# A ring of seven PSUM banks shared by scores and mean transposes, V loaded whole for the last tile, and one shared tile for the left-over keys

## The reference

```python
# first attention (L0), 4 heads of 32: only the 32 best keys of a row count
scores = einsum(Q, K) / sqrt(32)                 # 4 x 1024 x 6404
topv, topi = top_k(scores, 32)
attn = zeros.at[topi].set(softmax(topv))
attn_mean = attn.mean(axis=heads)                # 1024 x 6404
c_t = attn_mean @ V                              # 1024 x 128
...
# second attention (L1), 16 heads of 8: plain softmax over all 6404 keys
attn = softmax(q @ k.T / sqrt(8)); out = attn @ v
```

## Time and profile before

| | us |
|---|---|
| median of 3 runs | 2005.47 (2000.84 to 2008.52) |
| the profiled execution, its own time | 2001.17 |
| its span in the trace | 1999.4 |
| loop of the first attention | about 205 to 861 of the span |
| second attention | about 1076 to 1809 of the span |
| granted TensorE clock, mean | 0.9 |

### The profile page before, as it was taken

One profiled execution on the slowest core, in us unless ns is written; L12 is line 12 of the kernel. 1 busy time (PEld: TensorE's weight loads), 2 busy tenths in 40 slices (PEclk: granted clock), 3 DMA queues, 4 the chain that ended last, 5 costly groups with the idle time before them and its releaser, 6 DMA issues. The chain is left out here.

```text
span 1999.4 us, 22599 instructions
## 1 busy us (share of the span) xinstructions
PE 1590.6 (80%) x8229; PEld 609.5 (30%) x8229; DVE 857.4 (43%) x2286; ACT 1387.5 (69%) x1382; POOL 177.6 (9%) x153
## 2 busy tenths in 40 slices
PE   4357978888788788356464999999999999995996
PEld 3236334445444455333220111111111111113332
DVE  5734699999899898836320000000000000003223
ACT  3471678778778787410224999999999999992432
POOL 2743021111111111100000000000000000000000
PEclk8566989999999999678666999999999999997998
DMA  2122086796786876767002000610070000003000
GB/s 86 51 92 97 11 163 150 165 209 144 172 193 136 196 166 157 167 110 113 21 12 37 1 1 1 56 14 1 7 64 1 1 1 1 1 1 91 0 0 11
DMA packets 91348, 145.08 MB, mean 73 GB/s; under 512 B 46704, under 2 KB 59465, under 8 KB 90433
## 3 DMA queue, kind: packets, MB, share of 16 engines
q0 software_dynamic: 13472, 75.53, 18.9%
q1 hardware_dynamic: 77328, 67.19, 15.7%
q10 hardware_dynamic: 432, 0.85, 0.1%
HBM read 54.15 MB, written 13.99 MB: 34 GB/s over the span
## 5 line engine op out<-in xcount | busy, mean ns | idle before, releaser
L1735 ACT ACTIVATE ex<-ps 128x1536 f32<-128x1536 f32 x544 | 731.2, 1496 | 1.2 <-PE ps L1694 1.0
L1707 PE MATMUL ps<-ex,V 128*9 128x512 f32 x3264 | 427.3, 596 | 0.2 <-ACT ex L1735 0.2
L753 PE MATMUL ps<-K,qst 128*128 128x512 f32 (+1 forms) x832 | 380.3, 601 | 20.6 <-ACT srow L819 14.7
L1694 PE MATMUL ps<-Q,K 52*128 52x512 bf16 x1632 | 328.9, 385 | 64.9 <-ACT ex L1735 33.3
L1745 DVE COPY o<-ps 9x512 f32<-9x512 f32 x32 | 22.0, 687 | 742.8 <-PE ps L1707 742.0
L947 DVE MAX8 cand<-srow 128x8 f32<-128x200 f32 (+1 forms) x1024 | 320.8, 363 | 8.0 <-ACT srow L819 8.0
L819 ACT COPY srow<-ps 128x1024 f32<-128x1024 f32 (+1 forms) x224 | 206.0, 922 | 98.8 <-PE ps L753 98.2
L907 DVE SCALAR_TENSOR_TENSOR both<-srow,top,both 128x1536 f32<-128x1536 f32 (+1 forms) x128 | 240.1, 1876 | 42.5 <-ACT both L835 42.3
L835 ACT ACTIVATE both<-srow,shift 128x1536 f32<-128x1536 f32 (+1 forms) x128 | 209.0, 1636 | 10.5 <-DMA both<-both 9.4
L753 PEld LDWEIGHTS ps<-K,qst 128*128 128x128 f32 x832 | 157.9, 201 | 177.1 <-issue 139.1
L1694 PEld LDWEIGHTS ps<-Q,K 52*128 52x128 bf16 x1632 | 60.2, 94 | 482.0 <-ACT ex L1735 446.8
(11 more groups left out here) (306 smaller groups left out, 1064.0 us busy)
## 6 DMA issues: line engine op xcount, KB each, us to landing
both<-both POOLq DMA_DIRECT2D x69, 768.0 KB, 8.8
v_ring<-v_rows SPq DMA_DIRECT2D x96, 256.0 KB, 3.9
both<-both POOLq DMA_DIRECT2D x23, 898.0 KB, 12.6
K<-k_parts SPq DMA_DIRECT2D x48, 204.0 KB
k_parts<-kl SPq DMA_DIRECT2D x12, 384.0 KB, 2.5
V<-v_rows SPq DMA_DIRECT2D x4, 918.0 KB, 30.8
v_rows<-v1g SPq DMA_DIRECT2D x12, 288.0 KB, 3.0
v_rows<-V SPq DMA_DIRECT2D x12, 256.0 KB, 3.2
```

Source lines behind the costliest of these rows:

```text
L753: last = M.matmul(ps[:, GBANK * (k % RING) + b, 0:c1 - c0], qst[:, h, :], K0[:, c0:c1], start=True, stop=True)
L1694: last = M.matmul(ps[:, n % 6, :], K1[rows_, quad % 2, hh // 2, g * P:(g + 1) * P], Q1[rows_, 4 * quad + hh, tb * TB:(tb + 1) * TB], start ...
L1707: last = M.matmul(ps[32 * j:32 * j + VW, 6 + w % 2, :], V1[:, quad % 2, g, VW * j:VW * j + VW], ex1[:, (4 * g + j) % NSLOT, :], start=g == ...
L1735: C.activation(ex1[:, n % NSLOT:n % NSLOT + NBANK, :], ps[:, n % 6:n % 6 + NBANK, :], ACT.Exp)\
```

## The change

1. **Ring.** Score groups and transposes share one ring of 7 banks. An order of all items (`ITEMS`: score group k, then the transposes that follow it) is written out at build time, with the bank of each (`BANK_OF`) and the number of items that ACT must have copied before it may be written (`FREE_AT`). While transposes follow every score group, this comes to: score group k waits for the copy of group k - 2; a transpose waits for the copy of a transpose or group at least one step back.
2. **Schedule.** The 13 transposes of tiles 0 to 5 follow 13 score groups in a row (offsets 3 to 15) instead of every second. `value_group` j comes 3 score groups behind its transposes (offsets 6 to 18), and `meanT` has 4 slots. `HURRIED` keeps its offsets for the transposes; its products also come 3 later.
3. **Whole V.** For tile 7 SP loads 50 tiles of V, 3.2 MB in rows of 25.6 KB, with one DMA into the slot of `srow` that turn 29 has freed. It stands in SP's queue ahead of the last two loads of tile 6, and waits for the last mask of turn 29. In the tail the transposes go up to 7 groups ahead, and the products run 3 groups behind them.
4. **Shared tile of keys.** In the second attention the 4 left-over keys of four heads share one tile, in 32 partitions each: 201 tiles and 67 units a pass. The last unit has 2 full score matmuls and 4 small ones; the last two value groups of a pass (49 and 50) fall into the same unit, unit 1 of the next pass. `load_quad` loads V in 1 + 4 DMAs.

```diff
-    RING = 3
+    RING = 7
+    MSLOTS = 4
+    VALUE_LAG = 3
+    TAIL_LAG = 3
-    SPREAD = [3, 5, 7, 9, 11, 13, 15, 17, 19, 21, 23, 24, 25]
+    SPREAD = list(range(3, 3 + NTURN))
...
+            TURN_AT[k] = (u, i)
+            VALUE_AT[k + VALUE_LAG] = (u, i)
+    ITEMS = []
+    for k in range(NI * NGRP):
+        ITEMS.append(("scores", k))
+        if k in TURN_AT:
+            ITEMS.append(("turn", TURN_AT[k]))
+    BANK_OF, FREE_AT, at, held = [], [], 0, {}
+    for n, (kind, k) in enumerate(ITEMS):
+        size = min(GBANK, NBK - (k % NGRP) * GBANK) if kind == "scores" else 1
+        if at + size > RING:
+            at = 0
+        BANK_OF.append(at)
+        FREE_AT.append(max(held.get(b, 0) for b in range(at, at + size)))
+        for b in range(at, at + size):
+            held[b] = n + 1
+        at += size
...
 def scores(n, g):
-                    if k >= RING:
-                        pe.wait_ge(S("evac"), k - RING + 1)
+                    if FREE_AT[item]:
+                        pe.wait_ge(S("evac"), FREE_AT[item])
...
 def turn_group(u, j):
-                    if m >= 1:
-                        pe.wait_ge(S("meanT_sb"), m if u < NT - 1 or j == 0 else m - 1)
+                    if u < NT - 1:
+                        pe.wait_ge(S("evac"), FREE_AT[ITEM_AT["turn", (u, j)]])
+                    elif j >= RING:
+                        pe.wait_ge(S("tail_copied"), j - RING + 1)
...
 for n in range(NI): for g in range(NGRP):
                         scores(n, g)
-                        mean_step(n * NGRP + g)
+                        k = n * NGRP + g
+                        if k in TURN_AT:
+                            turn_group(*TURN_AT[k])
+                        if k in VALUE_AT:
+                            value_group(*VALUE_AT[k])
...
 @block.sync
+                    if m == IN_TAIL - 2:
+                        sp.wait_ge(S("kept"), kept_by(LAST - 2, LOW))
+                        sp.dma_start(srow[:, (LAST - 2) % SLOTS, 0:(NG - 1) * P],
+                                     v0_rows[:, 0:NG - 1, :].rearrange("p n d -> p (n d)")).then_inc(S("v0_whole"), 16)
                     if m >= 2:
                         sp.wait_ge(S("summed"), m - 1)
...
 def load_quad
-        sp.dma_start(V1[:, b, :, :], v1_rows[:, :, quad * 4 * VW:(quad + 1) * 4 * VW]).then_inc(values_in, 16)
+        sp.dma_start(V1[:, b, 0:FULL1, :], v1_rows[:, 0:FULL1, quad * 4 * VW:(quad + 1) * 4 * VW]).then_inc(values_in, 16)
+        for j in range(4):
+            h0 = (4 * quad + j) * VW
+            sp.dma_start(V1[LEFT * j:LEFT * (j + 1), b, FULL1, 0:VW], v1_rows[0:LEFT, FULL1, h0:h0 + VW]).then_inc(values_in, 16)
...
-        NU = 4 * NG // NBANK
+        NTILE = 4 * FULL1 + 1
+        NU = NTILE // NBANK
...
 def scores(w, u)
+                        for hh in ([n % 4] if g < FULL1 else range(4)):
+                            if g < FULL1:
+                                out, col = ps[:, bank(w, n), :], 0
+                                keys = slice(g * P, (g + 1) * P)
+                            else:
+                                out, col = ps[LEFT * hh:LEFT * (hh + 1), bank(w, n), :], LEFT * hh
+                                keys = slice(g * P, g * P + LEFT)
```

More of the change, by code:

```diff
@@ L673, in program @@
         for i in range(NTURN):
[L674 to L676 removed]
+            k = first + (SPREAD if u < NT - 2 else HURRIED)[i]
+            TURN_AT[k] = (u, i)
+            VALUE_AT[k + VALUE_LAG] = (u, i)
+        SUMS_AT[k + VALUE_LAG + 1] = u
+    ITEMS = []
[3 more added lines that the diff above has]
+            ITEMS.append(("turn", TURN_AT[k]))
+    ITEM_AT = {item: n for n, item in enumerate(ITEMS)}
+    BANK_OF, FREE_AT, at, held = [], [], 0, {}
[8 more added lines that the diff above has]
+        at += size
     DEEP = 3
@@ L728, in edge_by, with evac_by, v0_tile @@
             return n * STEPS + 8
+        IN_TAIL = (NT - 1) * NTURN
         def turn_bank(m):
-            return 6 if m < (NT - 1) * NTURN else 5 + m % 2
+            return BANK_OF[ITEM_AT["turn", divmod(m, NTURN)]] if m < IN_TAIL else (m - IN_TAIL) % RING
+        def evac_by(k):
+            return ITEM_AT["scores", k] + 1
+        def v0_tile(u, c):
+            if u == NT - 1 and c < NG - 1:
+                return srow[:, (LAST - 2) % SLOTS, c * P:(c + 1) * P]
+            return v0_ring[:, (u * NTURN + c // 4) % 2, c % 4, :]
         def home_free(eng, n, c):
@@ L778, in value_group @@
                         w = min(P, G - c * P)
-                        last = M.matmul(ps[:, 7, 0:D], meanT[0:w, m % 2, (c % 4) * P:(c % 4 + 1) * P],
-                                        v0_ring[0:w, m % 2, c % 4, :], start=c == 0, stop=c == NG - 1)
+                        last = M.matmul(ps[:, 7, 0:D], meanT[0:w, m % MSLOTS, (c % 4) * P:(c % 4 + 1) * P],
+                                        v0_tile(u, c)[0:w, :], start=c == 0, stop=c == NG - 1)
                     last.then_inc(S("summed"), 1)
[L783 to L791, removed]
                 for n in range(NI):
@@ L817, in evac @@
                     act.wait_ge(S("scored"), n * NGRP + g + 1)
-                    b = GBANK * ((n * NGRP + g) % RING)
-                    C.copy(srow[:, n % SLOTS, g0:g1], ps[:, b:b + GBANK, :].rearrange("p a b -> p (a b)")[:, 0:g1 - g0])\
+                    b = BANK_OF[ITEM_AT["scores", n * NGRP + g]]
+                    C.copy(srow[:, n % SLOTS, g0:g1],
+                           ps[:, b:b + -(-(g1 - g0) // 512), :].rearrange("p a b -> p (a b)")[:, 0:g1 - g0])\
                         .then_inc(S("evac"), 1)
@@ L1179, in program @@
     KIN = 12
+    FULL1 = G // P
+    LEFT = 32
+    VIN = 1 + 4
+    assert NG == FULL1 + 1 and G - FULL1 * P <= LEFT
     oq, k1s = ExitStack(), ExitStack()
@@ L1706, in values @@
                     for j in range(4):
-                        last = M.matmul(ps[32 * j:32 * j + VW, 6 + w % 2, :], V1[:, quad % 2, g, VW * j:VW * j + VW],
-                                        ex1[:, (4 * g + j) % NSLOT, :], start=g == 0, stop=g == NG - 1,
-                                        tile_position=(0, 32 * j))
+                        out = ps[32 * j:32 * j + VW, 6 + w % 2, :]
+                        if g < FULL1:
+                            last = M.matmul(out, V1[:, quad % 2, g, VW * j:VW * j + VW], ex1[:, slot(w, 4 * g + j), :],
+                                            start=g == 0, stop=False, tile_position=(0, 32 * j))
+                        else:
+                            left = slice(LEFT * j, LEFT * (j + 1))
+                            last = M.matmul(out, V1[left, quad % 2, g, 0:VW], ex1[left, slot(w, NTILE - 1), :],
+                                            start=False, stop=True, tile_position=(LEFT * j, 32 * j))
                     last.then_inc(S("summed1"), 1)
```

106 lines of the change are left out of this document (63 added, 43 removed).

## The result

**Slower, by 1.3%.** The changed kernel takes 2030.91 us (median of 4 runs, 2024.38 to 2035.49) where the kernel before took 2005.4 (median of 4, 2000.84 to 2008.52): ratio 1.0127, 95% interval 1.0091 to 1.0162. I had forecast 2003, with a range of 1980 to 2023; this is the side of rival 2, between its 2019 and its 2036.

What follows compares the result with a forecast made beforehand. DVE was taken to set the pace in the first attention's turns 5 to 29, ACT in the second attention. Terms +3.8 - 2.6 + 5 - 7 - 3.8 + 2 = -2.6 us took the median 2005.5 to 2003; range 1980 to 2023.

Steps and rivals of the forecast that it cites:

- rival 2: Turns with consecutive steps: PE becomes the bound through late loads or half clock; 2019 to 2036 us, chance 0.30.
- the term +3.8: Six tiles, turns 5 to 29: new load stalls of 37.2 us against 33.4 us saved, net +3.8 us.
- The same stall is thus only moved: Six tiles: the old stall in turn 4u+7 moves to turn 4u+6, at 6.2 us a tile.
- 33.4 taken away and 37.2 added: Six tiles: the mean's 33.4 us cost to DVE goes; load stalls of 6.2 us a tile add 37.2.
- M(5) to M(29) over 483: Sign of rival 2: first masks of turns 5 and 29 start 483 us or more apart, against 470 forecast.
- Rival 1: Six tiles: loads of V get through the adds earlier, stall 3.4 us; total 1986 us, chance 0.33.
- Turns 29 to 31: +2.4 forecast: First mask of turn 29 to that of turn 31: -2.6 us and +5 us together, +2.4 us.
- The term of 5: Turns 29 to 31: whole V among the adds delays ACT's exponentials, +5 us, from 0 to 9.
- the term of -2.6: Turn 29 to 30: little mean work left and hurried loads in a quiet stretch, 18.05 for 20.7 us, -2.6 us.
- Tail: -7: From the last add to the first loop's end: transposes and first products already done, -7 us, between -10 and -4.
- Second attention: -3.8: Second attention: 8 fewer exponentials, -10.8 us, against ACT gaps of 6.0 and a later end of 1.0; -3.8 us.
- Loads for it: +2: Stage before the second attention: eight more small DMAs ahead of x_sb in SP's queue, +2 us, from 0 to 4.

Runs made afterwards that it cites:

- e2: Changed kernel with the old table of offsets, transposes after every second score group; 1975.23 us, ratio 0.9848 to the kernel before.
- e1: Changed kernel with the 89 ring loads of V left out, products reading two slots loaded once (computation incomplete); 1973.51 us, ratio 0.9853 to before.
- e10: Changed kernel with adds of every first added head cut to 8 columns a chunk (computation incomplete); 1964.2 us, ratio 0.9798 to before.
- e7: Changed kernel with the whole V issued behind the last load of tile 6 and the last mask of turn 30; 2027.75 us.
- e4: Kernel before with only the shared key tile added, including its loads of V in 1 + 4 DMAs; 2005.96 us, ratio 1.0011.
- e8: Changed kernel with the old table of offsets and x_sb loaded ahead of V and the keys; 1972.11 us, ratio 0.985 to before.
- e12: Changed kernel with the old table of offsets and the second attention of before; 1977.8 us, ratio 0.9872 to before.
- e3: Changed kernel with x_sb loaded ahead of the loads for the second attention; 2026.28 us, ratio 1.0138 to before.

## Why the prediction was wrong

1. **The stall of a tile: the term +3.8 measured +22.9.** This is the step that failed. I had put the new stall at 6.2 us a tile, 37.2 for six, over the 433.3 without a mean; it measured 489.6 - 433.3 = 56.3, or 9.4 a tile. The step was wrong in two places.
   - *Which load is late.* I followed products 8, 10 and 12 and let the odd loads through. The rows had the landing times about right (5.6, 9.4; measured 5.9, 7.6, 9.6, 7.9), but with a step of 3 us four loads in a row, 7 to 10, are issued into the adds. Load 9 took 9.6 us, and product 9 is the one ahead of the scores (8,2). I had put the stall on the last mask of turn 6, at 6.2 us; it came on the first, at 9.1 us in tile 0. The two half-clock pieces, 1.4 and 1.3 us in the scores alone, had no term, only a sentence.
   - *What the stall of before was.* "The same stall is thus only moved" was false. e2 shows that distance and ring alone take a tile from 77.8 to 73.6: the stall of before went with the lockstep, PE held by ACT's copies, and 4.2 of its 5.6 us a tile could be had with the old table. The new stall is another one, of loads among adds; against e2 the table without gaps costs 8.0 us a tile. I had both sides of the sum, 33.4 taken away and 37.2 added, but read them as one stall in a new place.
2. **Rival 2** named 2019 to 2036 us with the right kind of mechanism (late loads among products 9 to 12, a half-clock piece in each tile), though it too put the price on load 12 and not on load 9. Its sign was M(5) to M(29) over 483; measured 489.6. Its "PE becomes the bound" is refuted as such: with loads out of the way (e1, e10) PE's rate costs 1 us a tile at most.
3. **Rival 1** fell: no load issued from 328 to 340, among the adds of tile 0, took less than 5.9 us. I had also set beside it a rule of the Trainium skill (DMA: Bandwidth & Descriptors, Queues, rings and completion order), that each DMA engine goes round the queues for which it has work, a packet at a time. The page names no time for a load; that it would wait for about one add was my own reading of it. The trace disagrees with that reading in size: 7.6 and 9.6 us are 5.0 and 7.0 more than the 2.6 of a quiet load, one add taking 4.1 us of all engines.
4. **Turns 29 to 31: +2.4 forecast, +6.2 measured.** The mechanism was right: ACT's exponentials of turn 30 wait for adds twice, 5.61 and 5.65 us, where before it was once, 2.21, the add behind the whole V took 20.5 us, and the last load of tile 6 took 20.9 us. The whole V moved in 17.7 us. The term of 5 should have been about 9, the upper end that I gave; e7 gets just these 9 us back here, and its 32.8 us are 2.7 below before, as the term of -2.6 had it.
5. **Tail: -7, measured -7.7**: the mechanism was right, and from the end of the last add to the loop's end 882.1 - (869.09 + 2.03) = 11.0 us, forecast 12, before 18.7.
6. **Second attention: -3.8, measured -3.4.** Exponentials x536, and a gap at each of seven boundaries, as forecast. That the number fits is in part luck: the gaps are 0.57 to 0.65 us for 0.85, 4.2 in all for 6.0, and the last value group (1.0) lies behind the last exponential, where this stage ends; against that, one exponential took 722.3 / 536 = 1.348 us for 1.344, 1.9 us over all, and two gaps at the stage's start are some 1.4 us longer than before. ACT's timeline:

```profile
1207.54 90.25 ACT L1814 ACTIVATE ex<-ps 128x1536 f32<-128x1536 f32 x67 [0.57 <-PE ps L1768]
```

7. **Loads for it: +2, measured +13.1 in this pair of profiles.** Not settled. SP is held behind each of the two big loads of V in both kernels, 25.97 and 28.72 us before, 29.53 and 32.63 after, so 7.5 us of the 13 pass there. But kernels with the same code there took 97 to 106 us from the loop's end until SP was through (before: 97.3), and 117 to 123 from there to the first exponential (before: 118.5), so much of the 13 can be that spread; e4, the part alone, shows +7.5 in its profile and no difference in its median. The +2 for eight more issues is neither confirmed nor refuted.

The complete versions that beat both kernels are those with the old table: e8 at 1972.11 us, 1.5% under the kernel before, with e2 and e12 beside it.

## What to carry to other kernels

To close up a schedule takes away the slack of every transfer in it: before work is put in consecutive steps, follow each of its loads, odd and even ones, against the adds or stores that are under way at that moment, and look at what stands behind the waiting instruction on its queue. Two edits made together can hide one another (here -25 and +48 us in the same stretch), so a stall that "moves" should be tested by undoing one. A producer that runs several steps ahead of its consumer helps little in steps without gaps if the operand that comes by DMA has only two slots; with every second step left free, two slots were enough (e2).

## What the runs showed of the hardware

- A 256 KB load issued among the adds of a turn, three of 768 KB and one of 898, landed in 5.9 to 9.6 us in tile 0 of the changed kernel; with these adds cut to 4 KB, six loads in the same place took 2.6 (their median, e10): a factor of up to 3.7 on the same transfer.
- Right behind an idle piece of PE of 2.18 and of 3.02 us, the next scores ran at about half rate: 3.13 and 3.03 us for 1.72, at a granted clock of 0.54 and 0.57. Of the some 9 us that tile 0 lost, the waits are 5.2 and the clock most of the rest. Over the six tiles the granted clock is 0.92 in the changed kernel, 0.96 in e1 and 0.97 in e2 and before.
- The DMA issued right behind a load of 6400 or more rows of 144 bytes held SP's queue for 26 to 33 us before, in the changed kernel and in e3, whichever it was: a `mask_line` (25.97), `x_sb` (28.72), or the first of four loads of 4 keys (28 to 33). That the time belongs to the rows issued just before is argued from this; the number of rows was not varied.
- A load of 3.2 MB issued among the adds moved in 17.7 us; the add behind it landed after 20.5 us and a 192 KB load after 20.9.
